# Query and key projections of a gated cross-attention block: first bf16 part taken straight from PSUM, remainder by VectorE

## What is computed

```python
q  = heads(x @ Wq + bq);   k  = heads(x @ Wk + bk);   v  = heads(x @ Wv + bv)
qc = heads(x @ Wcq + bcq); kc = heads(ctx @ Wck + bck); vc = heads(ctx @ Wcv + bcv)
y  = softmax(causal(q @ k.T * scale)) @ v + softmax(qc @ kc.T * scale) @ vc
x  = x + tanh(g_xattn) * (y @ Wp + bp)          # 16 heads of 16 channels
```

## Time and profile before

| | before |
|---|---|
| device time, median of 3 runs | 1547.11 us (1543.27 to 1548.83) |
| span of the profiled execution, first to last instruction | 1501.5 us |
| mean granted TensorE clock over the span | 0.989 |
| PE busy | 1407.1 us (94%) |
| DVE busy | 1195.5 us (80%) |
| POOL busy | 902.8 us (60%) |
| ACT busy | 871.1 us (58%) |

### The profile page before, as it was taken

One profiled execution on the slowest core, in us unless ns is written; L12 is line 12 of the kernel. 1 busy time (PEld: TensorE's weight loads), 2 busy tenths in 40 slices (PEclk: granted clock), 3 DMA queues, 4 the chain that ended last, 5 costly groups with the idle time before them and its releaser, 6 DMA issues.

```text
span 1501.5 us, 36135 instructions
## 1 busy us (share of the span) xinstructions
PE 1407.1 (94%) x11224; PEld 947.2 (63%) x11288; DVE 1195.5 (80%) x3122; ACT 871.1 (58%) x1811; POOL 902.8 (60%) x1643
## 2 busy tenths in 40 slices
PE   3899999999999999999999999999988999999997
PEld 3456565565555665566555655655544899999775
DVE  6878798888888888888888878888855676787686
ACT  3466666666666666766666666666560566666210
POOL 4245466666747575666657475666655566776772
PEclk8999999999999999999999999999998999999999
DMA  6844455545464556455464546455573477565795
GB/s 173 203 134 131 136 153 160 147 139 178 129 169 136 154 140 178 130 150 177 118 181 130 154 139 170 142 156 153 152 227 137 138 228 231 172 178 175 251 342 168
DMA packets 184124, 250.01 MB, mean 167 GB/s; under 512 B 32025, under 2 KB 134561, under 8 KB 183937
## 3 DMA queue, kind: packets, MB, share of 16 engines
q1 hardware_dynamic: 149680, 185.60, 44.2%
q0 software_dynamic: 13008, 36.65, 6.8%
q10 hardware_dynamic: 21248, 25.46, 5.2%
HBM read 150.06 MB, written 95.97 MB: 164 GB/s over the span
## 4 chain that ended last, share of the span: by engine, by line
PE 64%; DVE 23%; issue 4%; ACT 4%; DMA 3%; POOL 1%; SPq 0%; DVEq 0%; POOLq 0%
DVE nmax L1261 10%; PE pv_self L1504 9%; PE vector_bank L2000 8%; PE scalar_bank L1440 8%; PE vector_bank L1477 6%; PE vector_bank L1550 3%; PE vector_bank L1414 3%; DVE q L1201 3%; PE vector_bank L1474 2%; PE scalar_bank L1427 2%; PE scalar_bank L1428 2%; PE scalar_bank L1430 2%; PE pv_cross L1486 2%; PE scalar_bank L1987 2%; PE pv_cross L2008 2%
## 5 line engine op out<-in xcount | busy, mean ns | idle before, releaser
L1261 DVE TENSOR_REDUCE nmax<-vector_bank 128x1 f32<-128x384 f32 (+4 forms) x832 | 509.1, 639 | 49.1 <-PE vector_bank L1477 45.1
L901 ACT ACTIVATE pt<-scalar_bank 128x512 f32<-128x512 f32 x640 | 361.1, 602 | 213.6 <-PE scalar_bank L1440 208.8
L731 POOL TENSOR_SCALAR_AFFINE_SELECT pt<-pt 128x256 f32<-128x256 f32 (+1 forms) x640 | 221.3, 360 | 205.9 <-ACT pt L901 184.0
L1440 PE MATMUL scalar_bank<-stack 99*64 99x512 bf16 (+4 forms) x1280 | 284.0, 319 | 1.8 <-ACT ct L901 0.6
L1477 PE MATMUL vector_bank<-stack 96*128 96x128 bf16 (+3 forms) x1024 | 244.2, 301 | 17.0 <-DMA stack<-qk_scratch 11.5
L1829 POOL DMA_INDIRECT rows<-pt x143 | 139.2, 973 | 80.4 <-issue 63.7
L1504 PE MATMUL pv_self<-pt,vst 128*32 128x512 f32 (+3 forms) x2048 | 161.0, 438 | 0.1
L690 POOL DMA_INDIRECT rows<-xn,slot x128 | 132.8, 1037 | 44.2 <-issue 26.3
L1474 PEld LDWEIGHTS vector_bank<-tri,ident_b 128*128 128x128 bf16 x704 | 66.8, 97 | 138.1 <-DVE nmax L1261 62.9
L1474 PE MATMUL vector_bank<-tri,ident_b 128*128 128x128 bf16 (+1 forms) x640 | 150.6, 235 | 2.5 <-DVE nmax L1261 0.8
L2000 PE MATMUL vector_bank<-pt 128*128 128x128 f32 x1144 | 151.3, 275 | 0.0
(11 more groups left out here) (320 smaller groups left out, 2834.4 us busy)
## 6 DMA issues: line engine op xcount, KB each, us to landing
qk_scratch<-parts SPq DMA_DIRECT2D x31, 1200.0 KB, 4.6
stack<-qk_scratch SPq DMA_DIRECT2D x120, 192.0 KB, 3.0
pt<-rows SPq DMA_DIRECT2D x143, 132.0 KB
stack<-qk_scratch SPq DMA_DIRECT2D x248, 72.0 KB, 2.6
stack<-qk_scratch SPq DMA_DIRECT2D x124, 128.0 KB, 3.1
stack<-qk_scratch SPq DMA_DIRECT2D x240, 36.0 KB, 2.2
pt<-rows SPq DMA_DIRECT2D x8, 1024.0 KB, 8.8
stack<-rows SPq DMA_DIRECT2D x8, 1024.0 KB, 11.4
```

Source lines behind the costliest of these rows:

```text
L731: pool.affine_select(out=v, in_=v, compare_op=ALU.is_ge, fill=0.0, base=0, pattern=pat, channel_multiplier=-1).then_inc(masked, 1)
L901: act.activation(dst, bank(kind, b, ("st", c, k))[:, :], ACT.Exp, scale=SCALE).then_inc(scalar_drained, 1)
L1261: dve.tensor_reduce(dst, src, axis=AX, op=ALU.max, negate=True).then_inc(vector_drained, 1)
L1440: return pe.matmul(out, stack[c][0:rows, head, key0:key0 + nk], stack[c][0:rows, head, q0:q0 + nq], start=True, stop=True, **kw)
```

## The change

ScalarE writes part 0 directly from PSUM with the bias added, and L842's fp32 copy and the cast L851 become this one instruction. VectorE makes the remainder from the bank itself: (bank + bias) - part 0, a scalar_tensor_tensor, into `rest`, which replaces `q32`. It waits for ScalarE's drain of that projection. The bank is now read twice, so PE waits, for a unit whose bank held a projection, also for the remainder (`r_ready`). ScalarE no longer waits for the previous split; VectorE does at i = 0. The wait for the scratch write now stands ahead of ScalarE's read of the bank.

```diff
+    def occupant(self, kind, b, name, ring):
+        at = self.names(kind).index(name) - ring
+        while at < 0:
...
+        return kind, b, self.names(kind)[at]
...
             def projected(kind, b, c):
-                if kind != "pro":
-                    act.wait_ge(split_done, n - 1)
                 for i, cols in enumerate(COLS):
                     act.wait_ge(scalar_filled, SU.upto(kind, b, ("proj", c, i)))
...
-                    act.activation(q32[:, cols], bank(kind, b, ("proj", c, i))[:, 0:cols.stop - cols.start], ACT.Identity,
-                                   bias=bias[:, 2 * i + c:2 * i + c + 1]).then_inc(scalar_drained, 1)
-                    act.wait_ge(scalar_drained, SU.upto(kind, b, ("proj", c, i)))
                     if kind == "pro" and c == 1 and i < 2:
                         act.wait_ge(cols_written[i], 16)
                     if i == (2 if kind == "pro" else 0) and n > 1:
                         act.wait_ge(scr_written, 16 * (n - 1))
-                    act.activation(parts[:, 0, cols], q32[:, cols], ACT.Copy).then_inc(h_ready, 1)
+                    act.activation(parts[:, 0, cols], bank(kind, b, ("proj", c, i))[:, 0:cols.stop - cols.start], ACT.Identity,
+                                   bias=bias[:, 2 * i + c:2 * i + c + 1]).then_inc(scalar_drained, 1)
...
             def subtract_part(kind, b, c, i):
-                dve.wait_ge(h_ready, 4 * SPLIT.upto(kind, b, c) - 3 + i)
-                dve.tensor_tensor(q32[:, COLS[i]], q32[:, COLS[i]], parts[:, 0, COLS[i]], ALU.subtract).then_inc(r_ready, 1)
+                n, cols = SPLIT.upto(kind, b, c), COLS[i]
+                dve.wait_ge(scalar_drained, SU.upto(kind, b, ("proj", c, i)))
...
+                elif n > 1 and i == 0:
+                    dve.wait_ge(split_done, n - 1)
+                dve.scalar_tensor_tensor(out=rest[:, cols],
+                                         in0=banks_s[SU.slot(kind, b, ("proj", c, i), RING)][:, 0:cols.stop - cols.start],
+                                         scalar=bias[:, 2 * i + c:2 * i + c + 1], in1=parts[:, 0, cols], op0=ALU.add,
+                                         op1=ALU.subtract).then_inc(r_ready, 1)
...
             def claim_s(kind, b, name):
                 n = SU.upto(kind, b, name) - RING
                 if kind != "pro" or n > 0:
                     pe.wait_ge(scalar_drained, n)
+                before_it = SU.occupant(kind, b, name, RING)
+                if before_it and before_it[2][0] == "proj":
+                    pe.wait_ge(r_ready, 4 * SPLIT.upto(before_it[0], before_it[1], before_it[2][1]) - 3 + before_it[2][2])
                 return banks_s[SU.slot(kind, b, name, RING)]
```

More of the change, by code:

```diff
@@ L60, in slot @@
         return (self.upto(kind, b, name) - self.credit - 1) % ring
+    def occupant(self, kind, b, name, ring):
+        at = self.names(kind).index(name) - ring
+        while at < 0:
+            if kind == "pro":
+                return None
+            kind, b = {"first": ("pro", 0), "mid": ("first", 0) if b == 1 else ("mid", b - 1),
+                       "last": ("mid", b - 1), "post": ("last", b - 1)}[kind]
+            at += len(self.names(kind))
+        return kind, b, self.names(kind)[at]
 PREV_UNITS = {(0, 1): ("yT", 0), (0, 2): ("yT", 1), (0, 4): ("wp", 0), (0, 5): ("wp", 1), (0, 6): ("wp", 2), (0, 7): ("wp", 3),
@@ L254, in attention_phase @@
         ctxT = sb("ctxT", [P, P])
-        q32 = sb("q32", [P, ALLC])
+        rest = sb("rest", [P, ALLC])
         parts = sb("parts", [P, 3, ALLC], BF16)
@@ L326, in attention_phase @@
         split_done = sem("split_done")
-        h_ready = sem("h_ready")
         r_ready = sem("r_ready")
@@ L379, in attention_phase @@
                       more_inputs=[flat[:, 0:KC * T].rearrange("p (k t) -> p k t", k=KC) for flat in (
-                          q32, xn2[0][:, :, :].rearrange("p t c -> p (t c)"), xn2[1][:, :, :].rearrange("p t c -> p (t c)"),
+                          rest, xn2[0][:, :, :].rearrange("p t c -> p (t c)"), xn2[1][:, :, :].rearrange("p t c -> p (t c)"),
                           late_raw)],
@@ L742, in low_parts @@
                 pool.wait_ge(m_ready, 4 * SPLIT.upto(kind, b, c))
-                pool.tensor_tensor(parts[:, 2, :], q32[:, :], parts[:, 1, :], ALU.subtract).then_inc(split_done, 1)
+                pool.tensor_tensor(parts[:, 2, :], rest[:, :], parts[:, 1, :], ALU.subtract).then_inc(split_done, 1)
             def body(kind, b):
@@ L857, in middle_part @@
                 act.wait_ge(r_ready, 4 * SPLIT.upto(kind, b, c) - 3 + i)
-                act.activation(parts[:, 1, COLS[i]], q32[:, COLS[i]], ACT.Copy).then_inc(m_ready, 1)
+                act.activation(parts[:, 1, COLS[i]], rest[:, COLS[i]], ACT.Copy).then_inc(m_ready, 1)
             def unnormalised(kind, b, w, c, g):
@@ L1198, in subtract_part @@
             def subtract_part(kind, b, c, i):
-                dve.wait_ge(h_ready, 4 * SPLIT.upto(kind, b, c) - 3 + i)
-                dve.tensor_tensor(q32[:, COLS[i]], q32[:, COLS[i]], parts[:, 0, COLS[i]], ALU.subtract).then_inc(r_ready, 1)
+                n, cols = SPLIT.upto(kind, b, c), COLS[i]
+                dve.wait_ge(scalar_drained, SU.upto(kind, b, ("proj", c, i)))
+                if kind == "pro" and c == 1:
+                    if i < 3:
+                        dve.wait_ge(low_ready, i + 1)
+                    else:
+                        dve.wait_ge(split_done, 1)
+                elif n > 1 and i == 0:
[4 more added lines that the diff above has]
+                                         op1=ALU.subtract).then_inc(r_ready, 1)
             def low_part(kind, b, c, i):
                 dve.wait_ge(m_ready, 4 * SPLIT.upto(kind, b, c) - 3 + i)
-                last = dve.tensor_tensor(parts[:, 2, COLS[i]], q32[:, COLS[i]], parts[:, 1, COLS[i]], ALU.subtract)
+                last = dve.tensor_tensor(parts[:, 2, COLS[i]], rest[:, COLS[i]], parts[:, 1, COLS[i]], ALU.subtract)
                 if i == 3:
```

## The result

The changed kernel takes 1573.13 us (median of 4 runs, 1572.0 to 1574.76); the kernel before took 1547.97 beside it. The ratio is 1.0169 (95% interval 1.0139 to 1.0199): 25 us slower. The direction was forecast, the size wasn't: 1561 was predicted, and the range ended at 1569.

What follows compares the result with a forecast made beforehand. PE was taken to bound the kernel, busy 65.33 of a batch's 68.15 us. 15 x (0.75 + 0.24) = 14.9, less 1.0 in the prologue, gave +13.9 on 1547.1: 1561.0 us, range 1544 to 1569.

Steps and rivals of the forecast that it cites:

- What bounds the kernel: In a mid batch PE is busy 65.33 of 68.15 us; an edit is worth its effect on the 2.82 idle.
- the wait for the bank: Projection stages: X1 waits for VectorE's remainder, so m6 is read 0.24 us later (c = 0), 0.75 (c = 1).
- The new subtraction: VectorE's remainder from PSUM with bias: 0.74 us for 512 columns in both stages, not stretched by GpSimd in c = 0.
- rival C: VectorE's new subtraction is stretched by GpSimd like the old one: +21.7 us, 1569; chance 0.10.
- Edits with no price: Other waits are already fulfilled, some units find banks free, GpSimd's L743 may start sooner with nobody waiting: no cost.
- I let the whole delay through: After m6 PE and DVE hold each other, so each batch keeps all of 0.75 + 0.24 us; bounds 0 to all.
- rival B: PE's other 2.4 us of idling, or a GpSimd and ScalarE lead, absorbs two thirds: +4 us, 1551; chance 0.19.
- The prologue: Two ScalarE casts leave the chain ahead of PE's wait for DMAs: 1.0 us less, once, between 0 and 1.27.
- The conversion from span to time: The median is 45.6 us above the profiled span of 1501.5, and that stays: 1547.1 us before the change.
- Rival A: The bank comes in time, so m6 waits only for DVE's queue: 16.9 us less, 1530; chance 0.13.

Runs made afterwards that it cites:

- e1: Changed kernel, VectorE's router subtraction moved from behind m6 in c = 1 to right behind the maximum, late in c = 0; 1562.7 us, ratio 1.0068.
- e6: Kernel before, casts and fp32 copy kept, only TensorE's new wait for the remainder added (bank held); 1598.1 us, ratio 1.0332.
- e5: Changed kernel, GpSimd's 3.23 us subtraction in c = 1 made to wait for VectorE's router subtraction; 1560.5 us, ratio 1.0048.
- e3: Changed kernel, TensorE's second score unit X1 emitted behind the cross products and m6 in both stages; 1538.6 us, ratio 0.9907.
- e10: Kernel before, TensorE's new wait added (bank held) and the router subtraction moved early, right behind the maximum; 1575.6 us, ratio 1.0128.

## Why the prediction was wrong in size

**What bounds the kernel, and the wait for the bank: right.** X1 starts late, and PE idles 1.13 us ahead of it in both stages ("some 1.2" was said). Counted from the start of the batch, m6 is read 0.30 late in c = 0 (0.24 forecast) and 0.68 in c = 1 (0.75 forecast). X1 in c = 0:

```profile
546.76 0.41 PE L1453 MATMUL scalar_bank<-stack 99*64 99x512 bf16 x2 [1.13 <-DVE rest L1208]
```

**The new subtraction: right.** 0.74 in both stages, and 0.27 for the 64 columns (min/median/max in ns of all of them):

```profile
L1208 DVE SCALAR_TENSOR_TENSOR rest<-scalar_bank,bias,parts x128: 272/741/750, 17.6 to 1067.7; 128x512 f32<-128x512 f32 x96, 128x64 f32<-128x64 f32 x32
```

In c = 0, where the earlier trace rows had 0.98, 0.86 and most of 1.10, DVE shows

```profile
542.51 0.74 DVE L1208 SCALAR_TENSOR_TENSOR rest<-scalar_bank,bias,parts 128x512 f32<-128x512 f32 x1
543.17 1.15 DVE L1271 TENSOR_REDUCE nmax<-vector_bank 128x2 f32<-128x512 f32 x2
544.23 0.74 DVE L1208 SCALAR_TENSOR_TENSOR rest<-scalar_bank,bias,parts 128x512 f32<-128x512 f32 x1
...
547.53 0.56 DVE L1271 TENSOR_REDUCE nmax<-vector_bank 128x1 f32<-128x384 f32 x1 [0.72 <-PE vector_bank L1490]
```

and GpSimd's row additions, between the same instants, take 2.79 in place of the 3.76 of the earlier trace rows:

```profile
542.85 2.79 POOL L770 TENSOR_TENSOR xr<-xr,bpg 128x256 f32<-128x256 f32 x4
```

So rival C is out.

**The step that failed** is in "Edits with no price": GpSimd's L743 "may start a little sooner, and no one waits for that". Nobody waits for it, but DVE is held up by it, at 1.33 us a batch (e1), which the sum put at nothing. Two shifts meet. In the kernel before, the two instructions stood like this; DVE's row, and GpSimd's:

```profile
567.63 0.22 DVE L1123 TENSOR_TENSOR logit<-logit,m 128x64 f32<-128x64 f32 x1
```

```profile
568.38 3.23 POOL L743 TENSOR_TENSOR parts<-q,parts 128x1600 bf16<-128x1600 f32 x1 [4.09 <-ACT parts L858]
```

Counted from the load of x that opens the batch (526.23 before, 537.70 after), GpSimd's start moves from 42.15 to 41.27, 0.88 sooner: the last middle part, which it waits for, ends 0.89 sooner on a ScalarE without casts. In e6, which keeps the casts, GpSimd starts no sooner (42.57). The row moves from 41.40 to 42.11, 0.71 later, since the held bank pushes m6 and what stands behind it. So 0.75 ahead became 0.84 behind. In e6 the held bank alone pushes the row to 42.82, 0.25 behind. The prediction had the second shift, and didn't lay it beside the first. e1, e5 and e3 each take the meeting apart in another way, and each time the row is short and the time goes.

The trace of the kernel before held the warning. These are the row in question and a second router row of the same shape (min/median/max ns):

```profile
L1123 DVE TENSOR_TENSOR logit<-logit,m x16: 213/217/225, 158.3 to 1143.6; 128x64 f32<-128x64 f32 x16
...
L1133 DVE TENSOR_TENSOR prob<-prob,z x16: 226/502/507, 161.9 to 1144.6; 128x64 f32<-128x64 f32 x16
```

Both read two SBUF operands over 64 columns. In the batch above, the 0.50 of L1133 began inside L743 (at 571.20, with L743 ending at 571.61) and ended 0.09 behind it. The prediction weighed the rule of the Trainium skill (SBUF — State Buffer, Who interferes with whom) for the new instruction alone, where it says that there is no contention. Of two SBUF inputs beside a GpSimd read, the same page of the Trainium skill (section SBUF: two separate sides) says that whichever starts first keeps the shared ports for its whole instruction; the trace agrees, with 2.47 us for a row of 0.22, done 0.08 behind the GpSimd instruction. It should have been put to every two-input row beside a GpSimd instruction that moves.

**"I let the whole delay through": too dear, and it hid the miss in part.** Without the collision (e1) a batch is 0.58 longer, not 0.99. c = 0 gives its delay back. PE waited there in the kernel before, 24.55 us into the batch, for the split maxima that GpSimd makes:

```profile
550.78 0.23 PE L1390 MATMUL vector_bank<-ident_b,mparts 128*96 128x128 bf16 x1 [0.38 <-issue]
```

In the changed kernel PE comes later and finds them ready, and this instruction is 0.22 earlier than its twin, although PE had been 0.33 late until then. So that part of rival B is right, for c = 0. GpSimd's shorter row additions aren't needed for it: e6 gives back the same 0.55 at the same place (0.87 late, then 0.32), with its additions as slow as before:

```profile
553.16 3.75 POOL L771 TENSOR_TENSOR xr<-xr,bpg 128x256 f32<-128x256 f32 x4
```

c = 1 begins 0.1 early in e1 and brings its transposed maxima to 0.73 late, of which 0.58 are left at the end of the batch. In the sum, 0.99 - 0.41 + 1.33 = 1.91 per batch: the forecast's mechanism with one term too large, and the larger term missing. e1's time, 10 us above its neighbour, would have been near the forecast of +13.9.

**The prologue:** the first batch, counted by its load of x, begins 0.85 earlier (54.44 instead of 55.29); 1.0 was forecast. That is partly luck. "Proj 3, X0 and the third score unit find their banks free" doesn't hold there: PE waits 6.05 for a remainder ahead of proj 3 of c = 1, and its wait for the DMAs then ends 2.73 sooner than the 36.17 of the earlier trace rows, not 1:

```profile
30.39 0.66 PE L1434 MATMUL scalar_bank<-ctxT,w_ck 128*128 128x64 f32 x2 [6.05 <-DVE rest L1208]
33.44 0.58 PE L1487 MATMUL vector_bank<-tri,ident_b 128*128 128x512 bf16 x1 [2.39 <-DMA stack<-qk_scratch]
```

Why 0.85 of it is left stays open. One pair can't tell it closely either: the six traces with the change have this load at 54.4 to 55.2, the five without at 54.9 to 56.7.

**The conversion from span to time was wrong**, as told above, but it did no harm: differences were added to the median of the runs.

**Rival A describes what the change is worth if the bank comes in time.** It put that at 1.06 us per batch and 16.9 in all. e3 has 1.04 per batch and 14 in all, and there m6 begins 0.49 earlier than in the kernel before in c = 0 (0.50 in rival A) and 1.04 in c = 1, 0.55 more (0.56). The bank doesn't come in time in e3, but m6 no longer stands behind X1. So the reading of DVE's queue and of the casts was right to that size, and what decided against the change is where X1 stands in TensorE's program.

## What to carry to other kernels

When an edit takes work from one engine, ask of each engine behind it which instruction will now start sooner, and lay that instruction beside the two-input VectorE rows near it: here a 0.2 us row that started inside a 3.2 us GpSimd instruction ended with it. Rows of one shape with different durations (0.22 and 0.50 here) can point to such a partner before any change is made. And before a buffer is held longer to save copies, move the work that doesn't need it ahead of the instruction that will wait: here that alone turned +25 us into -14.

## What the runs showed of the hardware that was not expected

A wait of TensorE can cost more than its own length: behind 1.41 us of idling, with PE busy for 0.47 of 2.10 us, the granted clock was 0.50 in the next stretch in some batches of the kernels with the bank held (e6 and e10). In e10 such a batch is 1.2 us longer. Behind the 1.13 us of the changed kernel the batch ran at 1.00. And the new form of the subtraction, with one operand in PSUM and a bias per row, took 0.74 for 512 columns, a little more than the 0.69 that the old one took when GpSimd didn't work beside it; by the earlier trace rows a value per row costs 53 ns and the PSUM operand nothing. But it kept its 0.74 beside GpSimd, which worked faster beside it as well: 2.79 us instead of 3.76 for its four row additions.
